# Two attribute products of a GAT kernel with an operand in PSUM, and a product with one-hots in four pieces

## The chip, the cores and the metric

The kernel runs on one core of a Trainium2 chip. The metric is the time on the device in microseconds, the median of the runs.

## The reference

Node rows x (3125 x 128) go through one graph convolution (two weights, the aggregate of a constant row by degrees) and then through five layers of graph attention with two heads. The graph has 50,000 edges, sorted by target, and one loop per node. A layer computes, cut to what matters here:

```python
edge_emb = edge_attr_full @ ew.T + eb
xw = x @ W
xj = xw[src].reshape(-1, H, D) + edge_emb.reshape(-1, H, D)
xi = xw[dst].reshape(-1, H, D)
alpha = jnp.einsum('ehd,hd->eh', xi, att_i) + jnp.einsum('ehd,hd->eh', xj, att_j)
alpha = jax.nn.leaky_relu(alpha, NEG_SLOPE)
amax = jax.ops.segment_max(alpha, dst, num_segments=N)
ea = jnp.exp(alpha - amax[dst])
denom = jax.ops.segment_sum(ea, dst, num_segments=N)
alpha = ea / (denom[dst] + EPS)
aggr = jax.ops.segment_sum(xj * alpha[..., None], dst, num_segments=N)
```

Each edge has 16 attributes. Their part of alpha is a product with a vector v of 16 per head, which is computed once per layer.

## The kernel before

Edges lie in tiles of 128, one edge per partition: 391 tiles, in 15 chunks (13 of K = 28 tiles, then 16 and 11), and in groups of four tiles (98 groups, seven in a full chunk). For each layer, each engine runs through the same order of tiles, and semaphores tie them together. There is no scheduler; the order is the order of the code.

- GpSimd issues one indirect gather per tile (L510), `table` rows by source node, into `ring`, which has 60 slots. From tile 60 on it waits for `sums` of the group that used the slot before. Its indices `srci` lie in SBUF.
- ScalarE copies, for each tile, 24 columns of the attention rows of both heads into `ai_win` (L580), and computes the exponentials of a chunk (L586).
- TensorE, in `aggregate`, clears a bank with a product of zeros (L741) and adds, for each tile, the product of the gathered rows with `pw` (L745) and of `est` with the one-hots (L747). At some groups it adds a product for the loops (L783, a self tile). It waits for `p_ready` from VectorE once per group.
- VectorE works on chunk c + 1 while TensorE aggregates chunk c. Ahead of the adds of the groups i = 0, 1 and 2 (`add_group`, L1200, which waits for `sums`) stand the parts 0, 1 and 2 of `windows_sum`: the attribute product `prod` (L1087), the product of `ai_win` with the one-hots (L1091), and both reductions (L1093 into `ee`, which lies in `bwd`; L1094 into `alpha`). `chain_scan`, behind the add of i = 2, waits for the chunk's gathers (L1105). `chain_rows` and `chain_cols` follow behind that of i = 3, `chain_probs` behind that of i = 5: the transpose of the exponentials into `probs` (L1170), the probabilities and flags into `est` (L1172, L1173), and the attributes times the probabilities into `est` (L1175). `weigh` (L1161) makes `pw` for a group, four groups ahead of the adds.

`link(ins)` lets VectorE wait until `ins` has ended; `mark(ins)` counts it only. All tiles here are in SBUF apart from the eight `bank`s in PSUM. Bank 7 serves only the start of a layer.

Of the kernel before, what the change touches and what calls it, by code (L numbers as in the profile page):

```python
# [5 lines left out]
ALU = mybir.AluOpType  # L6
# [4 lines left out]
AX = mybir.AxisListType.X  # L11

P = 128
# [3 lines left out]
H = 2  # L17
LAYERS = 5
FA = 16
# [6 lines left out]
WIN = 24  # L26
ROW = D + H
REG = 3
HF = H * FA
QD = 32  # L30
EC = HF + 2 * H
BIG = 1e30
# [3 lines left out]
QB = 32  # L36
# [10 lines left out]
TC = [sum(CH[:c]) for c in range(NC + 1)]  # L47
# [50 lines left out]
def program(nc, x, src_rows, src_key, src_flat, dst_col, dst_next_col, dst_flat, dst_first,  # L98
            attr, W1, b1, W2, b2,
            weights, weightsT, attT, edge_w, edge_b, edge_woT, biases, edge_bias, out):  # L100
    with ExitStack() as ctx:
        def sb(name, shape, dt=F32):
            return ctx.enter_context(nc.sbuf_tensor(name, shape, dt))

        def sem(name):
            return ctx.enter_context(nc.semaphore(name))
# [12 lines left out]
        onehot = sb("onehot", [P, TILES, WIN])  # L119
# [4 lines left out]
        prod = sb("prod", [P, H * K * FA])  # L124
# [7 lines left out]
        alpha = sb("alpha", [P, H, QB])  # L132
# [4 lines left out]
        probs = sb("probs", [P, H, QB])  # L137
# [19 lines left out]
        v17 = sb("v17", [P, LAYERS, H, FA + 1])  # L157
# [15 lines left out]
        ee = bwd[:, :, :].rearrange("p h e -> p (h e)")[:, 0:H * K]  # L173
# [3 lines left out]
        Bl = y[0:EC, :, :].rearrange("p b f -> p (b f)")  # L177
        nsT = prod[:, 0:NT * QD].rearrange("p (j n) -> p j n", n=QD)
        dump = prod[:, :].rearrange("p (b f) -> p b f", f=D)
# [81 lines left out]
        b2s = ai_win[:, :, :, :].rearrange("p k h w -> p (k h w)")[:, D:2 * D]  # L261

        bank = [ctx.enter_context(nc.psum_tensor(f"bank{i}", [P, 512], F32)) for i in range(8)]

        def gcn_sum(g):
            return bank[g % 3][:, 0:GW]
# [10 lines left out]
        step = sem("step")  # L277
# [58 lines left out]
        est_ready = sem("est_ready")  # L336
        acc_zero = sem("acc_zero")
        win_ready = sem("win_ready")
        win_used = sem("win_used")
# [182 lines left out]
        def ai_copy(copy, engine, layer, q, h):  # L522
            a, b = q * TQ * P, min(NP, (q + 1) * TQ * P)
            engine.wait_ge(ai_ps, H * NQ * layer + H * q + h + 1)
            copy(ai_rows[:, h, a:b], bank[4 + h][:, 0:b - a]).then_inc(ai_sb[h], 1)

        @block.scalar
        def _(act):
# [41 lines left out]
            def windows(layer, c):  # L570
                gc = layer * NC + c
                if gc:
                    act.wait_ge(win_used, gc)
                for g in GC[c]:
                    _, t, n = GROUPS[g]
                    _, base = nc.values_load_multi_w_load_instructions(
                        bases[0:1, t:t + n], engines=(mybir.EngineType.Activation,), min_val=0, max_val=LAST_BASE,
                        skip_runtime_bounds_check_because="clamped on the chip")
                    for k in range(n):
                        ins = nc.scalar.copy(ai_win[:, t - TC[c] + k, :, :], ai_rows[:, :, bass.ds(base[k], WIN)])  # L580
                ins.then_inc(win_ready, 1)
# [227 lines left out]
        def _(v):  # L809
            steps = [0]  # L810

            def mark(ins):
                steps[0] += 1
                ins.then_inc(step, 1)
                return steps[0]

            def link(ins):
                v.wait_ge(step, mark(ins))
# [5 lines left out]
            V = nc.vector  # L824
# [7 lines left out]
            link(V.tensor_scalar(phi_mask[:, 0:1], iota_p, float(FA), None, ALU.is_lt))  # L832
            link(V.tensor_scalar(phi_mask[:, 1:2], iota_p, float(HF), None, ALU.is_lt))
            link(V.tensor_tensor(phi_mask[:, 1:2], phi_mask[:, 1:2], phi_mask[:, 0:1], ALU.subtract))
            for h in range(H):
                link(V.tensor_scalar(mask_tmp[:, :], iota_p, float(HF + h), None, ALU.is_equal))
                link(V.tensor_tensor(phi_mask[:, h:h + 1], phi_mask[:, h:h + 1], mask_tmp[:, :], ALU.add))
# [109 lines left out]
            for c in range(NPC):  # L947
                pick(c, n_e)
                b, ne = c % 2, n_e[:, c * PC:(c + 1) * PC]
# [71 lines left out]
            for g in range(GCN_G):  # L1021
# [3 lines left out]
                c, i = divmod(g, K // GRP)  # L1025
# [13 lines left out]
                win = acc[:, 0, bass.ds(base[0], GW)]  # L1039
# [40 lines left out]

            def windows_sum(layer, c, part):
                gc, k, hk = layer * NC + c, CH[c], H * CH[c]
                ts = slice(TC[c], TC[c + 1])
                win, pr = ai_win[:, 0:k, :, :], prod[:, 0:hk * FA].rearrange("p (h k f) -> p h k f", h=H, f=FA)
                if part == 0:
                    v.wait_ge(at_in[gc % NAT], 16 * (gc // NAT + 1))
                    link(V.tensor_tensor(pr, at[:, gc % NAT, 0:k, :].unsqueeze(1).broadcast_to((P, H, k, FA)),  # L1087
                                         v17[:, layer, :, 0:FA].unsqueeze(2).broadcast_to((P, H, k, FA)), ALU.mult))
                if part == 1:
                    v.wait_ge(win_ready, gc + 1)  # L1090
                    link(V.tensor_tensor(win, win, onehot[:, ts, :].unsqueeze(2).broadcast_to((P, k, H, WIN)), ALU.mult))  # L1091
                if part == 2:
                    V.tensor_reduce(ee[:, 0:hk], prod[:, 0:hk * FA].rearrange("p (q f) -> p q f", f=FA), AX, ALU.add)  # L1093
                    link(V.tensor_reduce(alpha[:, :, 0:k].rearrange("p h k -> p k h"), win, AX, ALU.add))  # L1094
                    v.sem_inc(win_used, 1)
                    link(V.tensor_tensor(alpha[:, :, 0:k], alpha[:, :, 0:k],
                                         ee[:, 0:hk].rearrange("p (h k) -> p h k", h=H), ALU.add))

# [59 lines left out]
            def weigh(layer, g):  # L1158
                c, t, n = GROUPS[g]
                k = t - TC[c]  # L1160
                V.tensor_tensor(pw[:, g % DEEP, 0:n, :, :],  # L1161
                                onehot[:, t:t + n, :].unsqueeze(2).broadcast_to((P, n, H, WIN)),
                                est[:, c % 2, k:k + n, HF:HF + H].unsqueeze(3).broadcast_to((P, n, H, WIN)), ALU.mult)\
                    .then_inc(p_ready, 1)

            def chain_probs(layer, c):
                gc, k, hk = layer * NC + c, CH[c], H * CH[c]
                es = est[:, c % 2, 0:k, :]
                v.wait_ge(exp_al, gc + 1)
                link(V.transpose(probs[:, :, :], dd[:, 0:H * QB].rearrange("p (h e) -> p h e", h=H)))  # L1170
                pr = probs[:, :, 0:k].rearrange("p h k -> p k h")
                done = mark(V.tensor_copy(es[:, :, HF:HF + H], pr))  # L1172
                V.tensor_tensor(es[:, :, HF + H:EC], maxes[:, :, 0:k].rearrange("p h k -> p k h"),  # L1173
                                last_col[:, TC[c]:TC[c + 1]].unsqueeze(2).broadcast_to((P, k, H)), ALU.mult)
                V.tensor_tensor(es[:, :, 0:HF].rearrange("p k (h f) -> p k h f", h=H),  # L1175
                                at[:, gc % NAT, 0:k, :].unsqueeze(2).broadcast_to((P, k, H, FA)),
                                pr.unsqueeze(3).broadcast_to((P, k, H, FA)), ALU.mult).then_inc(est_ready, 1)
                v.wait_ge(step, done)
                for g in GC[c][0:2 if c else AHEAD]:
                    weigh(layer, g)  # L1180
# [22 lines left out]
            for layer in range(LAYERS):  # L1203
# [15 lines left out]
                for q in range(NQ):  # L1219
                    ai_copy(V.tensor_copy, v, layer, q, 1)  # L1220
                v.wait_ge(acc_zero, NT * (layer + 1) + 1)
                for part in range(3):
                    windows_sum(layer, 0, part)
                chain_scan(layer, 0)
                chain_rows(layer, 0)
                chain_cols(layer, 0)
                chain_probs(layer, 0)
                for c in range(NC):
                    more = c + 1 < NC
# [37 lines left out]
                v.wait_ge(added, G * (layer + 1))  # L1267
                for q in range(P // QD):
                    ins = V.transpose(nsT[q * QD:(q + 1) * QD, :, :],
                                      acc[QD:2 * QD, 2, 0:NP].rearrange("p (j q n) -> p q j n", q=P // QD, n=QD)[:, q, :, :])  # L1270
                link(ins)
# [21 lines left out]
                for j in range(NT):  # L1293
# [7 lines left out]
                    if not final and j >= 1:  # L1301
# [3 lines left out]
                    ins = V.scalar_tensor_tensor(out=yj, in0=yb[:, D:2 * D], scalar=c1[:, 1, j:j + 1],  # L1305
                                                 in1=yj, op0=ALU.mult, op1=ALU.add).then_inc(y_sb, 1)
# [71 lines left out]
```

## Time and profile before

| | us |
|---|---|
| median of 3 runs | 3388.77 |
| lowest and highest | 3386.15, 3389.04 |
| span of the profiled execution | 3764.7 |
| TensorE busy | 2439.0 (65%) |
| VectorE busy | 2004.0 (53%) |
| GpSimd busy | 2210.5 (59%) |
| ScalarE busy | 696.7 (19%) |

The profiled execution has no time of its own beside its span, and the span is 376 us longer than the median of the runs, which were made without a profile. Durations come from this one execution.

### The profile page before, as it was taken

What the parts mean: (1) busy time and instruction counts of PE and PEld (TensorE: products, weight loads), DVE (VectorE), ACT (ScalarE), POOL (GpSimd) and SP (SyncE); (2) the same over time, 40 slices, a digit from 0 to 9 for tenths busy, and PEclk for the clock granted to TensorE, in tenths of its full rate; (3) what the DMA queues carried; (4) which work ended last, traced back from release to release, by engine and by line L of the source; (5) the groups of instructions that cost most, each with busy time, mean ns of one, the idle gap of its engine ahead of it and who ended that gap; (6) DMA issues with size and microseconds to landing.
All of it is one profiled execution on the core that took longest, in us unless ns stands there. A gap on an engine that the chain in (4) does not pass through costs nothing.

```text
span 3764.7 us, 48376 instructions
## 1 busy us (share of the span) xinstructions
PE 2439.0 (65%) x13595; PEld 2001.4 (53%) x13595; DVE 2004.0 (53%) x6216; ACT 696.7 (19%) x3102; POOL 2210.5 (59%) x2357
## 2 busy tenths in 40 slices
PE   6779726666582766658276665837576582766668
PEld 6679615555461655547165554725455461655546
DVE  8955624554472555547255554725454472555456
ACT  0078511111121111112111111211111121111112
POOL 0067466666626766662666666266676626666661
PEclk8555555555565555556555555655555565555556
DMA  3212122222202222221222222022222202222221
GB/s 101 97 60 80 30 52 54 53 52 57 49 24 51 54 51 53 56 49 30 47 54 52 53 56 49 25 53 54 50 53 57 50 24 50 54 50 53 52 49 40
DMA packets 114121, 195.78 MB, mean 52 GB/s; under 512 B 39897, under 2 KB 77272, under 8 KB 113864
## 3 DMA queue, kind: packets, MB, share of 16 engines
q0 software_dynamic: 62560, 130.25, 15.2%
q1 hardware_dynamic: 51304, 62.42, 5.3%
q8 instruction: 122, 2.00, 0.2%
q14 instruction: 135, 1.11, 0.1%
HBM read 180.86 MB, written 11.67 MB: 51 GB/s over the span
## 4 chain that ended last, share of the span: by engine, by line
DVE 36%; PE 25%; another core or an unknown queue 20%; issue 13%; DVEq 3%; POOL 1%; ACT 1%; ACTq 1%; DMA 0%; POOLq 0%
PE bank L745 10%; PE bank L747 6%; DVE acc L1200 4%; DVE into L1143 2%; DVEq L1016 2%; PE bank L718 2%; DVE pw L1161 2%; DVE alpha L1094 2%; PE bank L741 2%; PE bank L783 2%; DVE fwd L1150 2%; DVE lanes L1129 2%; DVE prod L1072 1%; PE bank L766 1%
## 5 line engine op out<-in xcount | busy, mean ns | idle before, releaser
L510 POOL DMA_INDIRECT ring<-table,srci x1955 | 1941.2, 993 | 937.6 <-issue 556.4
L745 PE MATMUL bank<-pw,ring 128*128 128x48 f32 x3910 | 1210.9, 404 | 203.3 <-issue 201.8
L745 PEld LDWEIGHTS bank<-pw,ring 128*128 128x128 f32 x3910 | 1014.9, 314 | 302.9 <-issue 231.1
L1200 DVE TENSOR_TENSOR acc<-acc,bank 128x288 f32 x490 | 222.8, 455 | 1128.7 <-remote 857.3
L747 PE MATMUL bank<-onehot,est 128*36 128x24 f32 x3910 | 632.6, 243 | 222.9 <-issue 221.7
L741 PE MATMUL bank<-zeros 128*128 128x288 bf16 x490 | 208.5, 426 | 697.1 <-DVE pw L1161 438.7
L747 PEld LDWEIGHTS bank<-onehot,est 128*36 128x36 f32 x3910 | 391.2, 149 | 393.9 <-issue 226.6
L741 PEld LDWEIGHTS bank<-zeros 128*128 128x128 bf16 x490 | 55.4, 113 | 752.0 <-DVE pw L1161 453.3
L586 ACT ACTIVATE dd<-dd 128x66 f32<-128x66 f32 x75 | 19.4, 258 | 2163.4 <-DVE dd L1154 1177.9
L580 ACT COPY ai_win<-ai_rows 128x48 f32 x1955 | 336.3, 229 | 432.6 <-issue 410.5
L491 POOL TENSOR_TENSOR ring<-ring,acc 128x512 f32<-128x512 f32 x98 | 117.1, 1195 | 250.1 <-ACT ring L545 246.7
L517 POOL TENSOR_TENSOR S<-S 128x128 f32<-128x128 f32 x125 | 57.4, 459 | 323.6 <-ACT S L590 319.2
L783 PE MATMUL bank<-Wl,S 128*128 128x258 f32 x250 | 152.8, 697 | 50.1 <-issue 48.7
L718 PE MATMUL bank<-onehot,ring 128*128 128x24 f32 x784 | 172.2, 388 | 18.4 <-ACT ring L556 7.9
L718 PEld LDWEIGHTS bank<-onehot,ring 128*128 128x128 f32 x784 | 169.3, 331 | 21.1 <-DVE bank L1043 8.8
L1091 DVE TENSOR_TENSOR ai_win<-ai_win,onehot 128x1344 f32<-128x1344 f32 (+2 forms) x75 | 109.1, 1455 | 122.5 <-issue 101.2
L1161 DVE TENSOR_TENSOR pw<-onehot,est 128x192 f32<-128x192 f32 x490 | 160.0, 352 | 0.1
L556 ACT ACTIVATE ring<-ring,acc 128x128 f32<-128x128 f32 x392 | 124.3, 389 | 29.4 <-PE bank L718 24.7
L1143 DVE COPY into<-carry 2x96 f32<-2x96 f32 x300 | 93.6, 312 | 45.9 <-issue 33.8
L800 PE MATMUL bank<-El,acc 128*128 128x256 f32 x250 | 95.8, 470 | 23.8 <-DVE y L1305 20.0
L1094 DVE TENSOR_REDUCE alpha<-ai_win 128x56 f32<-128x1344 f32 (+2 forms) x75 | 108.6, 1448 | 0.0
L783 PEld LDWEIGHTS bank<-Wl,S 128*128 128x128 f32 x250 | 64.6, 308 | 70.3 <-issue 63.8
(214 smaller groups left out, 2610.1 us busy)
## 6 DMA issues: line engine op xcount, KB each, us to landing
ring<-table,srci POOLq DMA_INDIRECT x1955
ai_rows<-lo_dram SPq DMA_DIRECT2D x28, 896.0 KB, 4.3
at<-in_attr SPq DMA_DIRECT2D x65, 224.0 KB
table<-ring SPq DMA_DIRECT2D x15, 390.0 KB, 3.5
table<-ring SPq DMA_DIRECT2D x5, 325.0 KB, 3.4
result<-ring SPq DMA_DIRECT2D x24, 64.0 KB
x_mid<-ring SPq DMA_DIRECT2D x3, 384.0 KB, 2.7
table<-ring SPq DMA_DIRECT2D x5, 130.0 KB, 2.4
```

The source lines that it names most:

```text
L510: nc.gpsimd.indirect_dma_start(out=ring[:, slot(t), :], out_offset=None, in_=table, in_offset=bass.IndirectOffsetOnAxis(ap=srci[:, t:t + 1 ...
L556: ins = nc.scalar.activation(rows[:, g % 3, k, :], pre[:, g % 3, k, :], ACT.Relu, scale=n_e[:, t:t + 1])
L580: ins = nc.scalar.copy(ai_win[:, t - TC[c] + k, :, :], ai_rows[:, :, bass.ds(base[k], WIN)])
L718: ins = nc.tensor.matmul(total[:, at_k], rows[:, g % 3, k, :], onehot[:, t0 + k, :], start=False, stop=k == GRP - 1, skip_group_check=True)
L741: nc.tensor.matmul(total, zeros[:, 0:P], zeros[:, :], start=True, stop=False, skip_group_check=True)
L745: nc.tensor.matmul(wide[:, 0:H, at_k], ring[:, slot(t), 0:D], pw[:, g % DEEP, k, :, :], start=False, stop=False, skip_group_check=True)
L747: ins = nc.tensor.matmul(wide[0:EC, H, at_k], est[:, c % 2, t - TC[c], :], onehot[:, t, :], start=False, stop=k == n - 1, skip_group_check ...
L783: nc.tensor.matmul(bank[3][:, 0:H * D + H], S[:, j, D:2 * D], Wl[:, layer % 2, :], start=True, stop=True).then_inc(s_ps, 1)
L1094: link(V.tensor_reduce(alpha[:, :, 0:k].rearrange("p h k -> p k h"), win, AX, ALU.add))
L1143: ins = V.tensor_copy(into[i * QB:i * QB + H, :, :], carry[:, :, 1 + i:1 + P:NQB])
L1161: V.tensor_tensor(pw[:, g % DEEP, 0:n, :, :], onehot[:, t:t + n, :].unsqueeze(2).broadcast_to((P, n, H, WIN)), est[:, c % 2, k:k + n, HF:H ...
L1200: V.tensor_tensor(win, win, grp_sum(g).rearrange("p (r w) -> p r w", r=REG), ALU.add)\
```

## The change

Two views of bank 7 are new: `v_ps` holds v of both heads, `probs_ps` the probabilities of a chunk. The attribute product reads v from `v_ps`, into which it is copied once per layer. `chain_probs` copies `probs` into `probs_ps` and waits for this copy before the product of attributes and probabilities, which reads it there. The product of `ai_win` with the one-hots and its reduction are made in four pieces of k/4 tiles, a product one piece ahead of the reduction, all in part 1; part 2 keeps the reduction of `prod` and the sum, and now waits between them.

```diff
+        probs_ps = bank[7][:, 0:H * QB].rearrange("p (h e) -> p h e", h=H)
+        v_ps = bank[7][:, H * QB:H * QB + HF].rearrange("p (h f) -> p h f", h=H)
...
                     link(V.tensor_tensor(pr, at[:, gc % NAT, 0:k, :].unsqueeze(1).broadcast_to((P, H, k, FA)),
-                                         v17[:, layer, :, 0:FA].unsqueeze(2).broadcast_to((P, H, k, FA)), ALU.mult))
+                                         v_ps.unsqueeze(2).broadcast_to((P, H, k, FA)), ALU.mult))
                 if part == 1:
                     v.wait_ge(win_ready, gc + 1)
-                    link(V.tensor_tensor(win, win, onehot[:, ts, :].unsqueeze(2).broadcast_to((P, k, H, WIN)), ALU.mult))
+                    cuts = [k * q // WIN_PARTS for q in range(WIN_PARTS + 1)]
+
+                    def multiply(q):
+                        a, b = cuts[q], cuts[q + 1]
+                        return mark(V.tensor_tensor(win[:, a:b], win[:, a:b],
+                                                    onehot[:, TC[c] + a:TC[c] + b, :].unsqueeze(2)
+                                                    .broadcast_to((P, b - a, H, WIN)), ALU.mult))
+
+                    def add_up(q):
+                        a, b = cuts[q], cuts[q + 1]
+                        return V.tensor_reduce(alpha[:, :, a:b].rearrange("p h k -> p k h"), win[:, a:b], AX, ALU.add)
+
+                    done = multiply(0)
+                    for q in range(WIN_PARTS):
+                        following = multiply(q + 1) if q + 1 < WIN_PARTS else 0
+                        v.wait_ge(step, done)
+                        ins = add_up(q)
+                        done = following
+                    link(ins)
+                    v.sem_inc(win_used, 1)
                 if part == 2:
-                    V.tensor_reduce(ee[:, 0:hk], prod[:, 0:hk * FA].rearrange("p (q f) -> p q f", f=FA), AX, ALU.add)
-                    link(V.tensor_reduce(alpha[:, :, 0:k].rearrange("p h k -> p k h"), win, AX, ALU.add))
-                    v.sem_inc(win_used, 1)
+                    link(V.tensor_reduce(ee[:, 0:hk], prod[:, 0:hk * FA].rearrange("p (q f) -> p q f", f=FA), AX, ALU.add))
...
                 done = mark(V.tensor_copy(es[:, :, HF:HF + H], pr))
+                copied = mark(V.tensor_copy(probs_ps, probs[:, :, :]))
                 V.tensor_tensor(es[:, :, HF + H:EC], maxes[:, :, 0:k].rearrange("p h k -> p k h"),
                                 last_col[:, TC[c]:TC[c + 1]].unsqueeze(2).broadcast_to((P, k, H)), ALU.mult)
+                v.wait_ge(step, copied)
                 V.tensor_tensor(es[:, :, 0:HF].rearrange("p k (h f) -> p k h f", h=H),
                                 at[:, gc % NAT, 0:k, :].unsqueeze(2).broadcast_to((P, k, H, FA)),
-                                pr.unsqueeze(3).broadcast_to((P, k, H, FA)), ALU.mult).then_inc(est_ready, 1)
+                                probs_ps[:, :, 0:k].rearrange("p h k -> p k h").unsqueeze(3).broadcast_to((P, k, H, FA)), ALU.mult).then_inc(est_ready, 1)
...
                 v.wait_ge(acc_zero, NT * (layer + 1) + 1)
+                link(V.tensor_copy(v_ps, v17[:, layer, :, 0:FA]))
```

On VectorE, between the add of a chunk's sixth group and the first `weigh` of the next chunk (`chain_probs`), there stood in the kernel before:

```order
L1170 STREAM_TRANSPOSE probs<-dd 128x64
L1172 COPY est<-probs 128x28x2
L1173 TENSOR_TENSOR est<-maxes,last_col 128x28x2
L1175 TENSOR_TENSOR est<-at,probs 128x28x32
L1161 TENSOR_TENSOR pw<-onehot,est 128x192 x2
```

and there stands in the changed kernel:

```order
L1190 STREAM_TRANSPOSE probs<-dd 128x64
L1192 COPY est<-probs 128x28x2
L1193 COPY bank<-probs 128x64
L1194 TENSOR_TENSOR est<-maxes,last_col 128x28x2
L1197 TENSOR_TENSOR est<-at,bank 128x28x32
L1181 TENSOR_TENSOR pw<-onehot,est 128x192 x2
```

A copy has come between the copy and the flags (`bank` is bank 7), and the product reads `bank` in place of `probs`.

On VectorE, from the product of `ai_win` with the one-hots (part 1 of `windows_sum`, ahead of the add of the group i = 1) to the end of part 2, there stood:

```order
L1091 TENSOR_TENSOR ai_win<-ai_win,onehot 128x1344
L1016 TENSOR_LOAD lanes
L1200 ISA
L1200 TENSOR_TENSOR acc<-acc,bank 128x3x96
L1161 TENSOR_TENSOR pw<-onehot,est 128x192
L1215 COPY node_ai<-bank 128x2
L1216 TENSOR_TENSOR S<-bank,ebl 128x256
L1093 TENSOR_REDUCE bwd<-prod 128x56
L1094 TENSOR_REDUCE alpha<-ai_win 128x28x2
L1096 TENSOR_TENSOR alpha<-alpha,bwd 128x2x28
```

and there stands now, up to the end of the work of the group i = 1:

```order
L1098 TENSOR_TENSOR ai_win<-ai_win,onehot 128x336 x2
L1104 TENSOR_REDUCE alpha<-ai_win 128x7x2
L1098 TENSOR_TENSOR ai_win<-ai_win,onehot 128x336
L1104 TENSOR_REDUCE alpha<-ai_win 128x7x2
L1098 TENSOR_TENSOR ai_win<-ai_win,onehot 128x336
L1104 TENSOR_REDUCE alpha<-ai_win 128x7x2 x2
L1020 TENSOR_LOAD lanes
L1222 ISA
L1222 TENSOR_TENSOR acc<-acc,bank 128x3x96
L1181 TENSOR_TENSOR pw<-onehot,est 128x192
L1237 COPY node_ai<-bank 128x2
L1238 TENSOR_TENSOR S<-bank,ebl 128x256
```

The one product of 1344 elements has become four of 336, and the reduction over `ai_win` has come forward in four pieces, ahead of this add instead of behind it; the reduction into `bwd` (`ee`) and the sum into `alpha` follow as before.

## Rows read from the trace of the kernel before

**Rows 1.** Windows: preparation, first gather stage, up to the next, behind the last.
```profile
0.00:475.50 475.50, 378.56 (x4045) 344.74 (x4046) 337.94 (x781) 199.68 (x651) 176.21 (x177) 0.57 0.22 74
475.50:1042.30 566.80, 332.02 (x1518) 264.63 (x1517) 265.11 (x820) 74.75 (x403) 389.33 (x391) 0.51 0.22 52
1042.30:1133.20 90.90, 78.81 (x388) 65.00 (x389) 68.04 (x282) 26.58 (x92) 20.46 (x51) 0.67 0.09 25
...
3677.00:3765.00 88.00, 71.75 (x362) 60.67 (x361) 63.53 (x210) 17.27 (x64) 11.41 (x25) 0.66 0.14 39
```
The columns are the stretch, its length, and the busy time (with the number of instructions) of TensorE's matmuls, its weight loads, VectorE, ScalarE and GpSimd, then the granted clock, the DMA engines' share and GB/s.

**Rows 2.** Waits: engine and line, released by, us in total, times, longest.
```profile
POOL ring L510 <- issue: 556.4, 1825, 0.3
POOL ring L510 <- remote: 288.6, 113, 8.4
...
PE bank L747 <- issue: 221.7, 220, 3.3
PE bank L745 <- issue: 201.8, 214, 2.6
...
POOL ring L510 <- PE bank L747: 53.7, 12, 12.8
```

**Rows 3.** Groups: form, count, busy us, mean ns, idle before.
```profile
L510 POOL DMA_INDIRECT ring<-table,srci x1955 | 1941.2, 993 | 937.6 <-issue 556.4 <-remote 288.6 <-PE bank L747 53.7
...
L1200 DVE TENSOR_TENSOR acc<-acc,bank 128x288 f32 x490 | 222.8, 455 | 1128.7 <-remote 857.3 <-PE bank L747 158.7 <-issue 47.6
L1161 DVE TENSOR_TENSOR pw<-onehot,est 128x192 f32<-128x192 f32 x485 | 158.5, 352 | 0.1
L1091 DVE TENSOR_TENSOR ai_win<-ai_win,onehot 128x1344 f32<-128x1344 f32 x65 | 100.8, 1551 | 122.3 <-issue 101.2 <-ACT ai_win L580 21.1
...
L1087 DVE TENSOR_TENSOR prod<-at,v 128x896 f32<-128x896 f32 x65 | 71.0, 1093 | 5.2 <-remote 1.8 <-DVE acc L1191 1.4
L1175 DVE TENSOR_TENSOR est<-at,probs 128x896 f32<-128x896 f32 x65 | 70.5, 1084 | 0.0
```

**Rows 4.** Timeline of TensorE: start, length, instruction, idle before it.
```profile
1462.15 0.45 PE L741 MATMUL bank<-zeros 128*128 128x288 bf16 x1
...
1465.59 0.42 PE L741 MATMUL bank<-zeros 128*128 128x288 bf16 x1
...
1476.42 0.26 PE L747 MATMUL bank<-onehot,est 128*36 128x24 f32 x2 [1.17 <-issue]
```

**Rows 5.** The page's first line.
```profile
span 3764.7 us, 48376 instructions
```

**Rows 6.** Timeline of GpSimd, single gathers.
```profile
560.02 0.94 POOL L510 DMA_INDIRECT ring<-table,srci  x1 [8.38 <-remote]
...
1465.88 1.16 POOL L510 DMA_INDIRECT ring<-table,srci  x1 [0.30 <-issue]
...
1469.88 0.95 POOL L510 DMA_INDIRECT ring<-table,srci  x1 [0.31 <-issue]
...
1492.67 1.76 POOL L510 DMA_INDIRECT ring<-table,srci  x1 [0.30 <-issue]
...
1701.08 0.94 POOL L510 DMA_INDIRECT ring<-table,srci  x1 [0.30 <-issue]
```

**Rows 7.** Timeline of VectorE.
```profile
1464.67 1.55 DVE L1091 TENSOR_TENSOR ai_win<-ai_win,onehot 128x1344 f32<-128x1344 f32 x1
...
1468.82 1.54 DVE L1094 TENSOR_REDUCE alpha<-ai_win 128x56 f32<-128x1344 f32 x1
...
1492.52 1.09 DVE L1175 TENSOR_TENSOR est<-at,probs 128x896 f32<-128x896 f32 x1
1493.52 0.62 DVE L1161 TENSOR_TENSOR pw<-onehot,est 128x192 f32<-128x192 f32 x2
...
1748.14 0.46 DVE L1200 TENSOR_TENSOR acc<-acc,bank 128x288 f32 x1 [2.12 <-PE bank L747]
```

**Rows 8.** The gathers' line: shortest, median and longest in ns.
```profile
L510 POOL DMA_INDIRECT ring<-table,srci x1955: 942/947/2335, 475.5 to 3675.6; - x196
```

More of the change, by code:

```diff
@@ L29 @@
 HF = H * FA
+WIN_PARTS = 4
 QD = 32
@@ L1082, in windows_sum @@
                 gc, k, hk = layer * NC + c, CH[c], H * CH[c]
-                ts = slice(TC[c], TC[c + 1])
                 win, pr = ai_win[:, 0:k, :, :], prod[:, 0:hk * FA].rearrange("p (h k f) -> p h k f", h=H, f=FA)
```

## The prediction

> **What bounds the kernel now.** I read the profiled execution first by stages [rows 1]: 475.5 us of preparation and graph convolution, then five layers. A layer is a gather stage of some 567 us (566.8 in the first), in which GpSimd issues 391 indirect gathers, and about 91 us from the last gather's end to the next layer's first (90.9; 88.0 behind the last). TensorE's granted clock is 0.51 in the gather stage, the 1.2 GHz level, and VectorE is busy for under half of it.
>
> Next, who waits in a gather stage [rows 2]. GpSimd has two kinds of idle time before a gather: 556.4 us over 1825 gathers, 0.305 us each, which follow every gather, and 288.6 + 53.7 = 342.3 us in 125 waits for room in the ring, which TensorE's sums give free. Less the 0.305 us that each would have anyway these are 304 us. With a mean of 0.993 us per gather [rows 3] the queue alone needs 391 x (0.993 + 0.305) = 507.5 us per layer. So in the trace GpSimd is not quite the bound: it is held back by 304 us in five layers.
>
> What holds it back is TensorE, and that looks like a product of the tracing. TensorE idles 201.8 + 221.7 = 423.5 us inside groups, where the program has no wait [rows 2]. One sees it in [rows 4]: a group of four tiles takes 1465.59 - 1462.15 = 3.44 us when nothing intervenes, but elsewhere each one or two matmuls are preceded by 1.1 to 1.2 us of "issue". Dense, a layer would need 98 x 3.44 = 337 us of groups and 25 self tiles, far below 507.5.
>
> The median of the runs is 3388.77, the span 3764.7 [rows 5], 376 more. An estimate for a run in which GpSimd never waits: 3764.7 - 304 = 3461. The lag also shrinks. In the trace the last add of a layer ends 46.6 us after the last gather (1701.08 + 0.94 to 1748.14 + 0.46, [rows 6, 7]), because TensorE is a full ring behind. With TensorE abreast only about six groups (20.6 us) and one VectorE chain remain, which I put at 12 us (VectorE is busy for 265.11/15 = 17.7 us per chunk [rows 1], the larger part of it in this chain): 33 us. Five times 14 to 16 gives 75 less: 3386, beside a measured 3388.77. **So the runs that are timed are bound by the gather queue**, and each microsecond taken from a gather counts.
>
> **What slows a gather.** The median is 0.947 us and the smallest 0.942 [rows 8], the mean 0.993 [rows 3]. The sum above the median is 1941.2 - 1955 x 0.947 = 89.8 us. Gathers and VectorE side by side [rows 6, 7] say when. The gather that starts at 1492.67 takes 1.76 us; L1175, which reads two SBUF tiles, runs from 1492.52. Take an occupied time of 896/0.96 = 933 ns plus some 24: it ends at 1493.48, 0.81 behind the gather's start, and 0.81 + 0.947 = 1.76. The gather at 1465.88 takes 1.16: L1091 started at 1464.67, 1.40 + 0.024 later is 1466.09, 0.21 behind the gather. L1094, with one SBUF input and 1.54 us long, runs from 1468.82; the gather that starts inside it at 1469.88 takes 0.95. So a gather that starts inside a VectorE instruction with two SBUF inputs waits for its end, and one with a single SBUF input costs nothing.
>
> A rule of the Trainium skill speaks against a gain. "SBUF — State Buffer", section Who interferes with whom, says that tensor_tensor with both inputs in SBUF contends with GpSimd's reads alone, and infers that generating descriptors needs only the write side, as a probe saw no stalled DMA under tensor_tensor. By that inference the sum would be zero; the trace disagrees for this indirect gather (1.76 against 0.947), while the same section's rule on reads agrees with it.
>
> **The change, part by part.**
>
> *1. Both attribute products get an operand in PSUM.* Of 150 instructions, 130 have 896 elements [rows 3]. Occupied time h = 0.957; a gather starts every 1.249 us, so with even phases the mean stall is h²/(2 x 1.249) = 0.367; 130 x 0.367 + 10 x 0.124 + 10 x 0.061 (512 and 352 elements) = 49.5 us. This goes to zero. By [rows 3] the PSUM operand costs VectorE nothing: L1200 with 288 elements, one operand in PSUM, takes 455 ns, L1161 with 192, both in SBUF, 352, and 96 elements at 0.96 per ns are 100 of the 103.
>
> *2. The one-hot product in four.* Whole, h = 1.424: 0.812 x 65 + 1.8 = 54.6 us by the same formula. A quarter has 336 elements, h = 0.374, stall 0.056, four of them 0.224, 75 chunks 16. Saved 39.
>
> *Check of the formula.* It gives 49.5 + 54.6 + 9.8 (490 of L1161, h = 0.224) = 114 us where the trace has 89.8, 0.79 of it. In the trace the ring waits tie the phases of both engines together; in a run without them the phases differ. Thus 88.5 x 0.79 = 70 us by the trace, 88.5 by even phases. I take 80, between them, as the trace's lock is partly that of its own waits. The bounds: 49.5 x 0.79 = 39 if the quarters save nothing, and about 125 if gathers mostly fall early into the three instructions (the phases may lock again, to the landing for which VectorE waits at L1105).
>
> *3. What VectorE gets in addition, per chunk.* Starts of two L1161 lie 0.62 - 0.35 = 0.27 apart for 0.20 of elements [rows 7], so each further instruction costs 0.07: eight pieces take 8 x 0.42 = 3.36 where two took 1.47 + 1.55, +0.34. The copy of the probabilities and the wait for it: by L1161's and L1200's fixed part of 152 ns, a copy of 64 elements takes about 0.22; it runs beside L1173, +0.13 before L1175 and the two `weigh` behind it, for which TensorE waits at a chunk's start. The attribute sum now ends in a wait of its own, +0.1. Together 0.57, times 75 43 us. They lie in the 1128.7 us that VectorE idles before L1200 [rows 3]. The reduction, moved from ahead of the third add to ahead of the second, holds up the second add and one `weigh`, four groups ahead of TensorE, by 1.5 us of a group's 3.44. Without that cover the price is the whole 43. On the path that ends last (last landing to last add) is one chunk's copy, 0.13, five times: 0.7. The copy of v, 0.25 x 5, is in the layer's start, where GpSimd has 60 free slots, 75 us of gathers, ahead of the first sum. The trace shows one wait there, 8.38 us before 560.02 [rows 6]; where it stays in a timed run too, chunk 0's saving (1/15, 5 us) is lost and 0.8 us a layer added.
>
> By "VectorE: DVE Perf Modes" of the Trainium skill, section on the TRN2 errata, a PSUM source costs 62 cycles more per instruction than an SBUF source. That would be 150 x 0.065 = 10 us more of VectorE time; L1200 beside L1161 doesn't show it.
>
> Sum: 3388.8 - 80 + 1 = 3310.
>
> **The rivals.**
> *Absorbed (0.11).* The timed runs too are bound by TensorE and VectorE, as the trace is, and faster gathers only wait longer for the ring. For it: the trace's own 304 us. Against: the estimate of 3386, and 507.5 us of gathers which the time can hardly undercut. Time 3382 to 3395; 3389.
> *Slower (0.09).* VectorE's chain from landing to `weigh` sets the chunk's time (TensorE waits for pw at L741), with the additions of 0.57 in each chunk: 3389 + 43 = 3432, or + 10 if only the 0.13 before `weigh` count. It decides from where the VectorE-TensorE round exceeds 28 x 1.298 = 36.3 us; TensorE's seven groups and three self tiles are about 27, VectorE's busy time in a stage is 265.11/15 = 17.7, and they overlap.
> *The stall stays (0.05).* If what blocks is the length of the instruction or its write and not the second SBUF input, PSUM changes nothing and only the quarters save, about 31: 3359. Against: L1094.
> *Forecast (0.75).* 3262 to 3350 by the bounds of 39 and 125.
>
> **How the numbers follow.** Absorbed is mostly "same", its edges split. A change under 0.2% is what this measurement can't tell from none. Faster 0.75 + 0.05 + 0.01 = 0.81, same 0.09, slower 0.10. The range, 3262 to 3384, holds the forecast and the stall that stays, and leaves out the absorbed and slower cases and a saving over 125.
>
> **What will show it.** In the profile after: L510's mean falls from 993 to about 955 with the same median; gathers that start inside the two attribute products take 0.95; those inside a quarter at most 1.33. The profiled span falls less than the median, as the freed time partly turns into ring waits (over 342 us); the 0.305 between gathers stays. L1175 and L1087 keep 1.09 us, VectorE's busy time rises by some 30 us. The prediction is wrong if gathers beside the PSUM products are still long, if L510's mean falls and the median doesn't (then the queue wasn't the bound), or if TensorE's waits for pw grow.

## The result and the profile after

The changed kernel takes 3300.82 us (3300.07 to 3301.30, 4 runs), the one before 3387.91 beside it: a ratio of 0.9745 with a 95% interval of 0.9731 to 0.9759, 87 us less. The forecast was 3310 in a range of 3262 to 3384, with 0.81 for faster.

The profile of the changed kernel has a span of 3298.3 us, the time of its runs. The page's first line and the group of the gathers [rows 3]:

```profile
span 3298.3 us, 48906 instructions
...
L514 POOL DMA_INDIRECT ring<-table,srci x1955 | 1866.0, 954 | 632.8 <-issue 583.9
```

The windows of the first layer and of what follows the last gather (length, busy times, granted clock, as in [rows 1]):

```profile
475.60:967.60 492.00, 343.02 (x1607) 276.30 (x1605) 284.57 (x964) 70.26 (x406) 373.06 (x391) 0.51 0.26 60
967.60:1040.70 73.10, 60.65 (x298) 50.46 (x298) 56.11 (x244) 26.12 (x91) 20.43 (x51) 0.69 0.11 31
3228.50:3298.30 69.80, 55.35 (x286) 47.24 (x285) 50.35 (x167) 16.81 (x63) 11.38 (x25) 0.70 0.17 48
```

A gather stage lasts 492.0 us. Its 391 gathers are busy for 373.1 us of it, and 390 gaps of 0.305 between them are 118.9, together 492.0: GpSimd never stops in it. The waits say the same. VectorE now waits 676.9 us for gathers to land, where the first profile had 8.3, and no wait of the gathers for the ring of [rows 2] is left but 10.4 us that are the usual gap:

```profile
DVE alpha L1125 <- DMA ring<-table,srci: 676.9, 65, 16.4
PEld bank L745 <- DVE pw L1181: 619.6, 70, 38.1
PE bank L745 <- DVE pw L1181: 611.0, 70, 37.9
POOL ring L514 <- issue: 583.9, 1916, 0.3
```

What the change does to one gather is seen where both attribute products run. VectorE's timeline, then GpSimd's, in one chunk, and the product `prod` of a later one:

```profile
1229.66 0.22 DVE L1193 COPY bank<-probs 128x64 f32<-128x64 f32 x1
1229.91 1.09 DVE L1197 TENSOR_TENSOR est<-at,bank 128x896 f32<-128x896 f32 x1
...
1237.74 0.49 DVE L1098 TENSOR_TENSOR ai_win<-ai_win,onehot 128x336 f32<-128x336 f32 x1
...
1374.62 1.09 DVE L1090 TENSOR_TENSOR prod<-at,bank 128x896 f32<-128x896 f32 x1
```

```profile
1230.35 0.94 POOL L514 DMA_INDIRECT ring<-table,srci  x1 [0.30 <-issue]
...
1237.84 1.21 POOL L514 DMA_INDIRECT ring<-table,srci  x1 [0.30 <-issue]
...
1375.12 0.94 POOL L514 DMA_INDIRECT ring<-table,srci  x1 [0.30 <-issue]
```

The gathers that start at 1230.35 and 1375.12, 0.44 and 0.50 behind the start of a product with an operand in PSUM, take 0.94 each. The one at 1237.84 starts 0.10 behind a quarter of the one-hot product, which still reads two SBUF tiles, and takes 0.27 more. The trace of the kernel before had 1.76 beside L1175 [rows 6, 7]. Over the whole trace of the changed kernel, 61 gathers start inside the 896-element products L1090 and 59 inside L1197 (within 0.957 of their start), and none takes over 0.947; at these same phases, by the prediction's formula for two SBUF inputs, they would lose an estimated 11.5 and 37.3 us.

### The profile page after: what moved, and what is told of

Read it like the earlier page. It is cut to its first block, busy times and chain, and to the rows that moved or that the text cites. A ratio compares the mean times of both kernels' runs of the same rounds, so it can differ in the third digit from the quotient of the medians.

```text
span 3298.3 us, 48906 instructions
## 1 busy us (share of the span) xinstructions
PE 2403.9 (73%) x13595; PEld 1979.7 (60%) x13595; DVE 2039.6 (62%) x6746; ACT 669.5 (20%) x3102; POOL 2134.9 (65%) x2357
## 4 chain that ended last, share of the span: by engine, by line
POOL 49%; issue 18%; DVE 16%; PE 13%; DMA 2%; DVEq 1%; ACT 1%; POOLq 0%; ACTq 0%
POOL ring L514 48%; PE bank L749 5%; PE bank L751 2%; PE bank L722 2%; DVE prod L1076 2%; DVE ring L851 2%; DMA ring<-table,srci 1%; POOL ring L495 1%; DVE ai_rows L944 1%; PE bank L745 1%; DVE y L1322 1%; DVE y L1328 1%; DVE acc L948 1%; DVE acc L1222 1%; DVE prod L1292 1%
## 5 line engine op out<-in xcount | busy, mean ns | idle before, releaser
L514 POOL DMA_INDIRECT ring<-table,srci x1955 | 1866.0, 954 | 632.8 <-issue 583.9
L745 PE MATMUL bank<-zeros 128*128 128x288 bf16 x490 | 209.6, 428 | 611.0 <-DVE pw L1181 611.0
L751 PE MATMUL bank<-onehot,est 128*36 128x24 f32 x3910 | 619.1, 246 | 0.0
L751 PEld LDWEIGHTS bank<-onehot,est 128*36 128x36 f32 x3910 | 382.6, 150 | 177.5
L1125 DVE TENSOR_TENSOR alpha<-alpha,ring 128x56 f32<-128x56 f32 (+7 forms) x75 | 18.1, 242 | 677.0 <-DMA ring<-table,srci 676.9
L584 ACT COPY ai_win<-ai_rows 128x48 f32 x1955 | 309.1, 228 | 57.9 <-issue 22.7
L1098 DVE TENSOR_TENSOR ai_win<-ai_win,onehot 128x336 f32<-128x336 f32 (+1 forms) x300 | 136.3, 475 | 22.5 <-ACT ai_win L584 22.4
L1104 DVE TENSOR_REDUCE alpha<-ai_win 128x14 f32<-128x336 f32 (+1 forms) x300 | 134.8, 470 | 0.0
L560 ACT ACTIVATE ring<-ring,acc 128x128 f32<-128x128 f32 x392 | 124.3, 389 | 29.3 <-PE bank L722 24.7
```

The costliest lines, as they stand in the source:

```text
L514: nc.gpsimd.indirect_dma_start(out=ring[:, slot(t), :], out_offset=None, in_=table, in_offset=bass.IndirectOffsetOnAxis(ap=srci[:, t:t + 1 ...
L745: nc.tensor.matmul(total, zeros[:, 0:P], zeros[:, :], start=True, stop=False, skip_group_check=True)
L751: ins = nc.tensor.matmul(wide[0:EC, H, at_k], est[:, c % 2, t - TC[c], :], onehot[:, t, :], start=False, stop=k == n - 1, skip_group_check ...
L1098: return mark(V.tensor_tensor(win[:, a:b], win[:, a:b], onehot[:, TC[c] + a:TC[c] + b, :].unsqueeze(2) .broadcast_to((P, b - a, H, WIN)), ...
L1104: return V.tensor_reduce(alpha[:, :, a:b].rearrange("p h k -> p k h"), win[:, a:b], AX, ALU.add)
```

## The experiments

All are compared with the kernel before on the same chip. "Stalls" is the gathers' busy time less 1955 times their median. The letters A to E name the explanations that the expectations set against each other. Where stalls are given per instruction, each lengthened gather of the whole trace was put down to the VectorE instruction whose end it waited for.

**1. The kernel before, a second profile.**

> The kernel before, unchanged, for a second profile. The first profile's span was 3764.7 us beside runs of 3388, the changed kernel's is 3298.3 beside 3301. Theory A (the gather queue is the bound, tracing held the other engines back in the first profile): a profile without that disturbance has a span of 3380 to 3392, no wait of L510 for the ring, layers of some 507 to 512 us of gathers, and gathers longer by 87 us in total than in the changed kernel's trace (mean near 0.998 us). Rival B (timed runs are held back by TensorE and VectorE as the first profile was): ring waits of over 100 us stay in a trace whose span is near 3388.

3388.07 us (ratio 1.0, 0.999 to 1.0009). Span, gathers and waits:

```profile
span 3383.5 us, 48376 instructions
...
L510 POOL DMA_INDIRECT ring<-table,srci x1955 | 1957.9, 1001 | 633.9 <-issue 569.6 <-DMA table<-ring 39.7 <-PE bank L747 24.7
```

```profile
DVE alpha L1105 <- DMA ring<-table,srci: 755.6, 65, 17.0
```

```profile
475.40:985.90 510.50, 344.34 (x1615) 277.42 (x1613) 279.41 (x868) 71.08 (x411) 391.62 (x391) 0.51 0.25 58
985.90:1057.90 72.00, 60.04 (x296) 49.55 (x296) 55.16 (x236) 25.32 (x85) 20.42 (x51) 0.71 0.11 32
```

This execution is as long as the runs, and in it GpSimd is the bound as the prediction had inferred: the stage is 510.5 us, VectorE waits 755.6 us for landings, and what is left of waits for the ring (24.7 us) is the usual gap, 0.3 at most. The execution of [rows 1 to 8], 376 us longer, was a disturbed one; the 423.5 us of "issue" inside TensorE's groups [rows 2, 4] are gone. The busy time of the gathers falls by 1957.9 - 1866.0 = 91.9 us with the change, the time by 87. The rest is outside the gather stages: from a layer's last gather to the next layer's first it is 73.1 us in place of 72.0, and 69.8 in place of 68.1 behind the last. Rival B falls. The stalls are 112.4 us: L1091 38.4, L1087 31.2, L1175 28.9, L1161 11.8. In the changed kernel they are 20.5: the quarters 12.8, `weigh` 5.5, both attribute products nothing. Most of the 2 us that are missing in both sums end with a scan that reads two SBUF operands (L1135, now L1155). The 130 gathers of the second profile of before that start inside the reductions L1093 and L1094, with one SBUF input, take 0.003 over the median at most.

**2. The PSUM operands alone** (`WIN_PARTS = 1`).

```diff
-WIN_PARTS = 4
+WIN_PARTS = 1
```

> The changed kernel with the one-hot product and its reduction in one piece (both at the second group), the two attribute products from PSUM. Theory A: only L1091's stalls come back, by the formula with even phases 54.6 - 16 = 39 us; time 3388 - 49 = 3339 (3325 to 3355). Rival C (what was saved comes from the pieces or from the earlier release of the attention windows, the PSUM operands do nothing): 3388.

3332.53 us, ratio 0.9836 (0.9820 to 0.9853), 56 less than before. Stalls 53.0, of which the whole one-hot product has 41.6.

**3. The four pieces alone.**

```diff
-                                         v_ps.unsqueeze(2).broadcast_to((P, H, k, FA)), ALU.mult))
+                                         v17[:, layer, :, 0:FA].unsqueeze(2).broadcast_to((P, H, k, FA)), ALU.mult))
...
-                copied = mark(V.tensor_copy(probs_ps, probs[:, :, :]))
...
-                                probs_ps[:, :, 0:k].rearrange("p h k -> p k h").unsqueeze(3).broadcast_to((P, k, H, FA)), ALU.mult).then_inc(est_ready, 1)
+                                pr.unsqueeze(3).broadcast_to((P, k, H, FA)), ALU.mult).then_inc(est_ready, 1)
```

The wait for the copy and the copy of v, once per layer, are left out too.

> The four pieces alone, all operands in SBUF as before, no copies. Theory A: 3388 - 39 = 3349 (3335 to 3365). Rival C: 3301, the whole gain.

3366.69 us, ratio 0.9937 (0.9921 to 0.9954), 22 less; this lies outside the 3335 to 3365 that was expected. The pieces still cost 15.3 us of stalls, as the formula has it (16), but the whole product had only 38.4 to give, not 54.6. Both parts gain; rival C falls.

**4. The same copy and wait, in SBUF.** `fwd` is free at that place.

```diff
-        probs_ps = bank[7][:, 0:H * QB].rearrange("p (h e) -> p h e", h=H)
+        probs_ps = fwd[:, :, :]
...
-                                         v_ps.unsqueeze(2).broadcast_to((P, H, k, FA)), ALU.mult))
+                                         v17[:, layer, :, 0:FA].unsqueeze(2).broadcast_to((P, H, k, FA)), ALU.mult))
```

> The changed kernel with the same copy of the probabilities and the same wait, but into an SBUF tile (fwd), and v read from v17 in SBUF. Theory A (the second SBUF input blocks the gathers): as the four pieces alone, 3349, gathers inside both attribute products long again. Rival D (the order, the waits and the extra copy move the instructions apart from the gathers): 3301. If VectorE's additional copy cost time, it would be slower than the four pieces alone by up to 10 us; theory A has 0.

3382.67 us, ratio 0.9985 (0.9975 to 0.9995). With the same instructions in the same order as the changed kernel, the two SBUF operands cost 82 us (on two chips; 81 by the ratios): rival D falls. But 3349 had been expected, and it is also 16 us slower than the four pieces alone, for which theory A as I had it has no reason. The trace has one: with the copy ahead of it the product with the probabilities starts 0.79 us behind the start of the transpose in place of 0.50 (medians), so that the first gather inside it comes 0.25 behind its start in place of 0.56, and its stalls are 43.3 us in place of 29.1 in experiment 3, while the other instructions' are within 1.1 us. The busy time of the gathers says the same: 1951.6 against 1936.7. So the phase at which VectorE meets the gathers is fixed, not spread evenly. Experiments 11 and 12 test that.

**5. One more product with two SBUF inputs, and 6. one more reduction with one.** Each is 80 us of additional VectorE time.

```diff
+                    link(V.tensor_tensor(pr, at[:, gc % NAT, 0:k, :].unsqueeze(1).broadcast_to((P, H, k, FA)),
+                                         v17[:, layer, :, 0:FA].unsqueeze(2).broadcast_to((P, H, k, FA)), ALU.mult))
```

```diff
+                    link(V.tensor_reduce(ee[:, 0:hk], prod[:, 0:hk * FA].rearrange("p (q f) -> p q f", f=FA), AX, ALU.add))
```

> The changed kernel with one more attribute product per chunk, ahead of the one that stays, with v from SBUF (two SBUF inputs, 896 elements, 1.09 us, 75 times 80 us of VectorE time). Theory A: gathers that start inside it are long again; by even phases 65 x 0.367 + 0.9 = 25 us, in all 3326, anywhere from 3301 to 3372 by the phase at which it meets the gathers, and the time rises by what L514's busy time rises. Rival E (VectorE's own time counts): 3381.

> The changed kernel with the reduction of prod made twice per chunk (one SBUF input, 896 elements, 1.08 us, again 80 us of VectorE time). Theory A: no stall and no change, 3301 within 5 us (the phases of the pieces may shift). Rival E: 3381.

3322.72 us with the product, ratio 0.9799 (0.9783 to 0.9815); 3308.37 with the reduction, 0.9756 (0.9740 to 0.9773). On this chip the kernel before took 3391.28, so I read the ratios beside 0.9745: about 18 us and 4 us more, the latter inside the intervals. As they stand, the times are 22 and 8 us above 3300.82, and 3308.37 lies 2 us above what was expected. The gathers' busy time rose by 15.6 and 3.5 us, the latter because the median gather took 0.947 us in place of 0.944; its stalls fell by 2.4 us. VectorE's own time counts for little (4 us by the ratios, 8 as the times stand; rival E would have 80), a second SBUF input does. Of the 15.6 the additional product itself stalls 11.7, less than the 25 of even phases; the quarters behind it, which it moves to a worse phase, lose 6.9 more (19.7 from 12.8), and `weigh` some 2 less.

**7. `weigh` from PSUM too, and 8. the same with seven pieces.**

```diff
-                                est[:, c % 2, k:k + n, HF:HF + H].unsqueeze(3).broadcast_to((P, n, H, WIN)), ALU.mult)\
+                                probs_ps[:, :, k:k + n].rearrange("p h k -> p k h").unsqueeze(3).broadcast_to((P, n, H, WIN)), ALU.mult)\
```

> The changed kernel in which the 490 products of weigh (192 elements) read the probabilities from PSUM too. Theory A: their stalls, 10.6 us in the second profile of before and part of the 20.5 us that the gathers still lose in the changed kernel, go: 3292 (3286 to 3300). If short instructions don't stall a gather: 3301.

> As before it, with the one-hot product in seven pieces of four tiles (192 elements, 0.224 us of stall at most). Theory A: even phases give 7 x 0.020 x 75 = 10.5 us of stalls in place of 16, so 5 us less than the version with four pieces, while VectorE has 6 x 0.07 x 75 = 32 us more to do, which costs nothing: 3287 (3282 to 3295). Rival E: 3324.

3299.81 us, ratio 0.9731 (0.9714 to 0.9747), and 3298.53, 0.9725 (0.9709 to 0.9741). The first is at the edge of what was expected, the second 4 us above it. `weigh` stalls no gather any more, and the stalls are 13.1 and 8.0 us, but the median gather took 0.947 us in both profiles in place of 0.944, which takes 6 us back, and against the changed kernel on another chip both are within the intervals. The changed kernel and the version with seven pieces were therefore measured beside each other on one chip, five runs each.

**9. The changed kernel, and 10. the seven pieces with `weigh` from PSUM, again.**

> The changed kernel again, on one chip with the three that follow: 3301 to 3304, and the same 20 us of stalls (L514 busy 1866 us).

> weigh from PSUM and seven pieces again, beside the changed kernel on one chip. Its gathers lost 8.0 us against 20.5, but their undisturbed time was 0.947 us against 0.944, which takes back 6. Theory A: 6 to 12 us below the changed kernel.

The changed kernel takes 3300.45 us (3300.14 to 3301.15), the version with seven pieces 3294.15 (3290.90 to 3295.63), 6.3 less, beside 3386.06 for the kernel before: ratios of 0.9745 (0.9732 to 0.9759) and 0.9727 (0.9714 to 0.9741). The intervals of the ratios overlap, the runs themselves don't. Stalls are 21.4 and 10.3 us, and the gathers' busy time is 1866.9 and 1855.8. The seven pieces are the fastest version here.

**11 and 12. The kernel before, with VectorE held back.** One reduction with one SBUF input, whose result nobody reads, stands ahead of the copy to `est`: 448 elements in experiment 11, 256 in experiment 12 (`n` below is 28 and 16). By the trace it holds back the copy by 0.65 and 0.45 us. Only the start of L1175 and all behind it moves, relative to the landing. What was expected comes from the second profile of before: its gathers and instructions, with the latter shifted.

```diff
+                link(V.tensor_reduce(ee[:, 0:n], prod[:, 0:n * FA].rearrange("p (q f) -> p q f", f=FA), AX, ALU.add))
                 done = mark(V.tensor_copy(es[:, :, HF:HF + H], pr))
```

> The kernel before with one more reduction with one SBUF input (448 elements, discarded) per chunk, which is waited for ahead of the copy to est and so holds back L1175 and the weigh behind it by about 0.65 us. Theory A with locked phases: in the second profile of before most gathers meet L1175 0.56 us behind its start and lose 0.40, those ahead of them start 0.69 before it; moved by 0.65, the gather ahead starts 0.05 before the product and the one behind it comes when it has ended, so L1175's 29 us of stalls go nearly altogether, L1087's and L1091's stay: 3388 - 30 = 3358 (3350 to 3370), a kernel faster by a delay. If stalls are a matter of even phases: 3388. If VectorE's chain counts: 3388 + 49 = 3437.

> As before it with 256 elements, a delay of about 0.45 us. Locked phases: the gather ahead now starts inside L1175, 0.1 us behind its start, and loses 0.85; stalls grow by about 14 us: 3402 (3395 to 3410), slower than the kernel before. Even phases: 3388. VectorE's chain: 3422.

The longer delay makes the kernel faster: 3364.64 us (3363.36 to 3367.23), ratio 0.9936 (0.9923 to 0.9950), 21 less. The shorter makes it slower: 3402.37 (3399.57 to 3405.21), ratio 1.0045 (1.0032 to 1.0059), 16 more, where 14 were expected. Neither even phases (no change) nor VectorE's own time (slower both times) gives two signs; locked phases do. The instruction and the gather beside it in the same chunk, VectorE's row and GpSimd's each time. Without a delay, in the second profile of before:

```profile
1253.04 1.08 DVE L1175 TENSOR_TENSOR est<-at,probs 128x896 f32<-128x896 f32 x1
```

```profile
1253.34 1.59 POOL L510 DMA_INDIRECT ring<-table,srci  x1 [0.30 <-issue]
```

With 0.45 us (the instruction is now L1176):

```profile
1257.18 1.08 DVE L1176 TENSOR_TENSOR est<-at,probs 128x896 f32<-128x896 f32 x1
```

```profile
1257.28 1.80 POOL L510 DMA_INDIRECT ring<-table,srci  x1 [0.30 <-issue]
```

With 0.65 us:

```profile
1248.05 1.08 DVE L1176 TENSOR_TENSOR est<-at,probs 128x896 f32<-128x896 f32 x1
```

```profile
1247.88 0.94 POOL L510 DMA_INDIRECT ring<-table,srci  x1 [0.30 <-issue]
1249.12 1.09 POOL L510 DMA_INDIRECT ring<-table,srci  x1 [0.30 <-issue]
```

Without a delay the gather starts 0.30 behind the product's start and loses 0.65 us. With 0.45 it starts 0.10 behind and loses 0.86. With 0.65 one gather starts 0.17 ahead of it and loses nothing, and the next comes 1.07 behind its start, when the product is over, and loses only 0.15 to `weigh`. Over the whole trace L1176's stalls are 40.7 and 5.9 us, beside 28.9 in the kernel before; those of the one-hot product are 38.7 in both, and of L1087 33.5 and 29.5.

## Why the prediction was right

- **The bound.** "The runs that are timed are bound by the gather queue": shown by the second profile and by experiments 5 and 6. The lag was estimated at 33 us; in the second profile of before the last add of a layer ends 30.1 us behind its last gather (30.1 to 30.5).
- **The mechanism.** A gather that starts within a VectorE instruction with two SBUF inputs waits for its end, one with an operand in PSUM costs nothing: shown by experiments 2, 4 and 5 and by the rows and counts above. By the Trainium skill, "SBUF — State Buffer", Who interferes with whom, a tensor_tensor with two SBUF inputs contends with a GpSimd instruction that reads SBUF. The traces agree if this gather reads its indices at its start, which I did not test apart. They disagree with the inference in the same section of the Trainium skill that a tensor_tensor leaves descriptor generation untouched: 122 gathers that start inside L1087 and L1175 of 896 elements, in the second profile of before, take 0.48 us more on average. By the same traces the PSUM operand costs VectorE nothing: both products take 1.087 us, where they took 1.093 and 1.084.
- **Attribute products, 49.5 by even phases (39 by the first trace).** Experiment 2 measured 56; their stalls were 31.2 + 28.9 = 60.1 in the second profile, 11 above even phases.
- **One-hot product, 39 (31).** Mis-sized: 22 alone, and 31 to 32 on top of the PSUM operands (3332.5 to 3300.8, on two chips). The quarters cost what the formula gave; the whole cost 38.4 where even phases have 54.6. The stalls of `weigh`, for which the sum saved nothing, fell from 11.8 to 5.5 without a change of its own. The stalls thus fell by 92, the time by 87, beside 88.5 by even phases and the 80 that I took. That the total is so close is partly luck: 11 us too little for the attribute products, 6 for `weigh` and 3 for the quarters (12.8 in place of 16) stand against 16 too much for the whole one-hot product. The factor 0.79 came from the disturbed trace; without the disturbance all stalls are 112.4 where the formula has 114.
- **VectorE's additional work, 43 us, hidden.** Its busy time rose from 2005.8 us in the second profile of before to 2039.6, and experiment 6 shows that even 80 us more of it cost about 4, or 8 as the times stand. But what hides it is not what I named: of the 1128.7 us of idle time ahead of the adds, undisturbed 310.3 are left; the cover is the 755.6 us in which VectorE waits for landings. The copy puts the product 0.13 us later, as estimated.
- **The +1.** Mis-sized: what lies outside the gather stages grew by some 7 us (the 1.1 and 1.7 of experiment 1, and 0.2 ahead of the first). The last add of a layer ends 31.8 us behind its last gather in place of 30.1; the PSUM operands alone have 31.6 there in the first layer, the pieces alone 31.1.
- **The layer's start** had no wait for the ring over 0.3 us in either undisturbed trace, so nothing was lost there.
- **Wrong was a sign to watch for:** I had the profiled span falling less than the median, and the freed time turning into waits for the ring. The span fell from 3764.7 to 3298.3 and those waits are gone, since only the first profile was a disturbed execution. TensorE's waits for `pw`, whose growth was to be a sign against the prediction, must be read the same way: they are 611.0 us beside 438.7 in the first profile, but 640.5 in the undisturbed one, from which they fell. The mean of a gather came out at 0.954 beside a forecast of about 0.955, but from 1.001 and not from 0.993.

## What to carry to other kernels

Where indirect gathers issued by GpSimd are the bound, look at the spread of their durations beside VectorE's timeline: what costs is a VectorE instruction with two SBUF inputs. By the sum for even phases its price grows with the square of its length; measured here, the one-hot product cost 38.4 us whole, 15.3 in four pieces and 7 to 8 in seven. Give such an instruction one operand from PSUM, or cut it; VectorE may have more to do for it as long as it waits for the landings. And where one engine waits for the other once per chunk, their phases are locked: a shift of 0.2 us, from 0.45 to 0.65, was worth 38 us here, 1.1%. So an edit that only moves instructions should be judged by the stalls and not by its own work.

## What was not expected of the hardware

The phases. A delay of VectorE by 0.65 us per chunk made the kernel 21 us faster, and one of 0.45 us made it 16 us slower. Also the first profiled execution itself: 376 us longer than the runs of the same kernel, with idle "issue" time of 0.5 to 1.2 us before single instructions of TensorE, ScalarE and VectorE; the second had a span of 3383.5 us. What disturbed it no run here shows. And the undisturbed gather takes 0.944 or 0.945 us in most of the profiles, but 0.947 in four: 3 ns times 1955 are 6 us, as much as the last improvement. What sets it no run here shows.
